# Scaling a tile of integers on VectorE: a product of two tensors, the scale read at stride zero, for the form with a scalar operand

## The reference

```python
def act_qdq(x):
    qmax = 2.0 ** (ACT_BITS - 1) - 1.0
    scale = jnp.maximum(jnp.max(jnp.abs(x)) / qmax, 1e-12)
    return jnp.clip(jnp.round(x / scale), -qmax - 1.0, qmax) * scale
...
x = act_qdq(x)
up = act_qdq(x @ lpbq_dequant(w_up).T)
gate = act_qdq(x @ lpbq_dequant(w_gate).T)
sig = fixed_qdq_u16(jax.nn.sigmoid(gate))
gate = act_qdq(gate * sig)
o = act_qdq(gate * up)
return o @ lpbq_dequant(w_down).T
```

## Time and profile before

| | us |
|---|---|
| median of three runs | 1259.4 |
| lowest and highest | 1258.11, 1260.34 |
| the profiled execution | 1256.11 |
| its span in the trace | 1254.3 |
| around the span | 1.8 |

### The profile page before, as it was taken

How to read it: one execution, slowest core, us unless ns; L and a number is a source line. 1 busy time by engine, 2 the same in 40 slices (tenths; PEclk the granted TensorE clock), 3 DMA queues, 4 the chain that set the end, 5 groups by cost and what they waited for, 6 DMA issues and landing times. The chain is left out here.

```text
span 1254.3 us, 28844 instructions
## 1 busy us (share of the span) xinstructions
PE 1137.2 (91%) x8658; PEld 843.2 (67%) x8658; DVE 1070.1 (85%) x2303; ACT 934.0 (74%) x3155; POOL 448.1 (36%) x463
## 2 busy tenths in 40 slices
PE   1589999999999999999999999999975998989498
PEld 1456666666667666766666766666543988778498
DVE  6259999999999999999999999999874559989698
ACT  1368888888888888888888888888742569855595
POOL 0223334433334433333433333443110007767343
PEclk9899999999999999999999999999986999999799
DMA  5000000000100000100000100010000000000133
GB/s 165 23 17 27 28 22 21 21 21 23 34 22 20 20 20 20 34 24 20 20 20 20 30 29 20 20 33 22 5 4 8 1 1 0 1 1 1 32 104 99
DMA packets 35059, 32.85 MB, mean 26 GB/s; under 512 B 4164, under 2 KB 34748, under 8 KB 35004
## 3 DMA queue, kind: packets, MB, share of 16 engines
q1 hardware_dynamic: 32704, 31.50, 8.4%
q10 hardware_dynamic: 2300, 0.66, 0.3%
HBM read 24.81 MB, written 7.34 MB: 26 GB/s over the span
## 5 line engine op out<-in xcount | busy, mean ns | idle before, releaser
L593 ACT ACTIVATE Px<-score 125x896 f32<-125x896 f32 x128 | 117.4, 917 | 89.4 <-PE score L1121 89.4
L574 ACT ACTIVATE Ps<-score,nmax_s 112x112 f32<-112x112 f32 x512 | 176.3, 427 | 4.0 <-DVE nmax_s L797 4.0
L585 ACT ACTIVATE Px<-score,nmax_h 125x112 f32<-125x112 f32 x512 | 172.6, 367 | 0.8 <-DVE nmax_h L790 0.8
L790 DVE TENSOR_REDUCE nmax_c<-score 125x8 f32<-125x896 f32 x128 | 136.2, 1064 | 13.6 <-PE score L1040 10.4
L574 ACT ACTIVATION_READ_ACCUMULATOR Ps<-score,nmax_s 112x1 f32 x512 | 144.3, 282 | 0.0
L759 DVE TENSOR_REDUCE Zc<-Px 125x8 f32<-125x896 f32 x128 | 137.9, 1077 | 5.7 <-ACT Px L593 2.1
L504 POOL TENSOR_TENSOR Kbd_hi<-Ks_hi,mask 128x448 fp32r<-128x448 f32 x64 | 63.9, 999 | 202.9 <-PE score L1040 137.5
L1132 PE MATMUL outX<-Px,Vn 125*32 125x224 f32 x1536 | 113.6, 368 | 7.2 <-DVE Vn L773 7.2
L585 ACT ACTIVATION_READ_ACCUMULATOR Px<-score,nmax_h 125x1 f32 x512 | 113.0, 221 | 0.0
L525 POOL TENSOR_TENSOR rstd<-vare,half 112x1 f32<-112x1 f32 x64 | 35.1, 548 | 177.0 <-DVE vare L882 177.0
L531 POOL TENSOR_TENSOR xb<-x_in,abo 112x256 f32<-112x256 f32 x32 | 23.7, 739 | 200.2 <-DVE r L868 200.2
(11 more groups left out here) (244 smaller groups left out, 3638.2 us busy)
## 6 DMA issues: line engine op xcount, KB each, us to landing
ctx_in<-in_ctx SPq DMA_DIRECT2D x32, 375.0 KB
x_in<-in_x SPq DMA_DIRECT2D x32, 112.0 KB, 2.0
x_scratch<-x SPq DMA_DIRECT2D x32, 112.0 KB, 1.9
x2T_all<-x_scratch SPq DMA_DIRECT2D x32, 112.0 KB, 2.1
out<-x2T_all SPq DMA_DIRECT2D x32, 112.0 KB, 1.9
raw_w_up<-in_w_up SPq DMA_DIRECT2D x1, 768.0 KB, 5.6
raw_w_down<-in_w_down SPq DMA_DIRECT2D x1, 768.0 KB, 7.4
raw_w_gate<-in_w_gate SPq DMA_DIRECT2D x1, 768.0 KB, 9.5
```

What stands on the lines that cost most here:

```text
L574: ins = act.activation(Ps[:, g, :], score[slot][0:L, h // QUAD, (h % QUAD) * L:(h % QUAD + 1) * L], ACT.Exp, bias=nmax_s[:, g:g + 1], accu ...
L585: ins = act.activation(Px[u % 2][:, h, :], score[SLOT_OF[f"C{u}"]][0:C, h // QUAD, (h % QUAD) * L:(h % QUAD + 1) * L], ACT.Exp, bias=maxim ...
L593: act.activation(Px[u % 2][:].rearrange("s (q h) l -> s q (h l)", q=2), score[SLOT_OF[f"C{u}"]][0:C, :, 0:QW], ACT.Exp).then_inc(exp_c, 1)
L790: dve.tensor_reduce(dst, score[SLOT_OF[f"C{u}"]][0:C, :, 0:QW].rearrange("s q (h l) -> s q h l", h=QUAD), AX.X, ALU.max, negate=True).then ...
```

## The change

In `glu_integers` DVE multiplies the tile by `glu_inv`, a column with one value for each partition. Before, that column is the scalar operand of a `tensor_scalar`. Now it is the second input of a `tensor_tensor`, an operand of the tile's shape that reads the same element again and again at stride zero. Both inputs and the output lie in SBUF; the types (int32 from `U`, f32 from `glu_inv`, int32 to `glu_q`), the wait and the semaphore stay.

```diff
             def glu_integers(g, h):
                 wait(dve, h_done, g * 2 + (h - 1))
-                dve.tensor_scalar(glu_q[h], half_of(products_of_U, g, h), tiny["glu_inv"][:, 0:1], None, ALU.mult)\
-                    .then_inc(glu_q_done, 1)
+                dve.tensor_tensor(glu_q[h], half_of(products_of_U, g, h),
+                                  tiny["glu_inv"][:, 0:1].rearrange("p (o n) -> p o n", o=1).broadcast_to([P, HG, GT]),
+                                  ALU.mult).then_inc(glu_q_done, 1)
```

## The result

The changed kernel takes 1269.87 us, the median of four runs (1269.3 to 1271.32); the kernel before took 1258.76 beside it (1257.91 to 1260.34). The ratio is 1.0089, with a 95% interval of 1.0071 to 1.0106: 11.1 us slower. The forecast was 1270.6 us: 1259.4, the median of the three runs known then, plus 11.2. With a fourth run that median is 1258.76.

The account below looks back on a forecast made before the run. The prediction took POOL and DVE in strict turns to bound the hidden pass. 14 steady tiles at 0.71 us (9.9) and +1.3 for the first two made +11.2, so 1259.4 became 1270.6 us, range 1266.5 to 1274.5.

Parts of the forecast that it names:

- The chain: Hidden pass: POOL and DVE take strict turns, 3.10 us POOL, 0.71 DVE, 0.19 handover, 4.00 a tile.
- The moving time: DVE's product in the hidden pass: moving part doubles from 0.70 to 1.40 us; 1.56 us alone.
- Standing behind POOL: Hidden pass: DVE's product, both inputs in SBUF, waits for POOL's instruction to end, then moves; chance 0.87.
- The sum: Hidden pass: 14 steady tiles at 0.71 us make 9.9, the first two tiles +1.3, in all +11.2 us.
- the first pair: DVE's products of tiles 0 and 1 in the hidden pass: together +1.3 us.
- POOL's first instruction: POOL's first product in the hidden pass: about 4.4 us long after the change.
- the granted clock near 1.00: PE in the hidden pass: new pauses about 1.0 us, so no fall of the clock expected.
- The first rival: Hidden pass: DVE's product runs beside POOL and PE becomes the bound; 9.2 us less, 1250.2 us; chance 0.05.
- PE can start tile 2 when ACT has read tile 0: Start of the hidden pass, if DVE runs beside POOL: PE begins tile 2 at 1103.66.
- The pace: PE in the hidden pass, if DVE runs beside POOL: 3.72 us a tile.
- ACT and PE wait for POOL more than before: Hidden pass: both wait longer but lose nothing; PE stands about 1.0 us of every 4.71.
- the second rival: Hidden pass: DVE and POOL share; -0.19 to +0.71 us a tile, halfway +0.3, 1264 us; chance 0.05.

Follow-up runs that it names:

- e3: Changed kernel with each DVE product preceded by the same product written to a spare place, doubling what DVE moves; 1292.8 us.
- e8: Changed kernel with four buffers in place of two for the integers of the up products; 1271.87 us, ratio 1.0105 to the kernel before.
- e9: Kernel before with four buffers in place of two for the integers of the up products; 1258.7 us, ratio 1.0006.
- e1: Changed kernel with the scale copied once into a PSUM word and read there at stride zero; 1251.88 us, ratio 0.9951 to the kernel before.
- e6: Changed kernel with POOL's product replaced by one of 24 elements and three fills, hidden tensor not computed; one run, 1254.72 us.
- e7: Scale read from PSUM, plus four buffers in place of two for the up products' integers; 1251.33 us, ratio 0.9939 to the kernel before.
- e5: Kernel before with POOL's product replaced by one of 24 elements and three fills, hidden tensor not computed; one run, 1258.7 us.
- e2: Changed kernel with the scale copied once into a full SBUF tile and read at stride one; 1270.07 us, ratio 1.0094 to the kernel before.

## Why the prediction was right, point by point

- **The chain** of POOL and DVE in turn, read from the earlier trace rows, held in all kernels with both inputs in SBUF: e3 shows that added time on DVE appears in full, e8 and e9 that ACT's room counts for nothing.
- **The moving time**: 1.56 us alone was forecast from the earlier trace rows, 1.549 to 1.551 measured; 1.42 behind POOL, 1.43 measured.
- **Standing behind POOL**: read from the short product Vn and taken over to an instruction ten times as long. e1 (the same instruction with one input elsewhere) and e6 (the same instruction beside a POOL that only writes) show that both inputs in SBUF and POOL's reading are what it takes.
- **The sum**: a gap of 1.61 was forecast for the loop, 1.60 measured, from 0.90 (1.49 from 0.79 in the tiles written out, which I had put with the others). 14 tiles x 0.70 is 9.8, the first pair 3.02 in place of 1.74 gives 1.28 (half of it ahead of POOL's first instruction, half within it): 11.1 in all. POOL's instructions in the loop were some 0.02 shorter, which leaves the 10.8 of the pass. 75.5 was forecast for the stretch. The medians differ by 11.1; part of that agreement is luck, as the stages around the pass differ by 2.4 us between the two profiled executions alone.
- **POOL's first instruction**: about 4.4 forecast, 4334 ns measured. POOL's idle time: 31 and 30.8.

Four readings were off, none of which entered the sum.

- I expected the granted clock near 1.00 in the pass. The pauses within the loop did leave it there, but I missed the one at the start. PE stood longer, for 3.26 us (1.98 before): ACT had to wait until POOL's lengthened first instruction had freed a buffer, at 1113.95, and only then emptied the bank and converted the next `x`. The clock then fell to 0.83 and 0.74 in two stretches of 4 us. It cost nothing, as PE had slack (e8, where PE has no such pause, takes as long). The pause and the clock in the changed kernel:

```profile
1117.23 0.46 PE L1634 MATMUL gbank<-xq_hi,w_upT_hi 128*128 128x448 f32 x1 [3.26 <-ACT xq_lo L1445]
...
1112.00:1116.00 4.00, 1.98 (x10) 1.51 (x9) 2.02 (x2) 1.96 (x2) 4.00 (x2) 1.00 0.00 0
1116.00:1120.00 4.00, 2.77 (x11) 2.51 (x12) 4.00 (x3) 2.42 (x3) 2.51 (x2) 0.83 0.00 0
1120.00:1124.00 4.00, 4.00 (x17) 3.66 (x16) 4.00 (x2) 1.18 (x1) 2.51 (x2) 0.74 0.00 0
```

- The first rival, L1573 beside POOL, is real (e1), but its price was too high: 9.2 us forecast, 6.6 in the pass, 5.8 between the medians. The step that failed is "PE can start tile 2 when ACT has read tile 0". PE was then still at tile 1, at the lower clock (1.7 us late in e7's profile), and in e1 it later stood for 2.37 us for ACT, which waited for a buffer that POOL's first instruction held. The pace erred the other way: 3.72 a tile, read from the gate pass, was 3.61 in e1, some 1.5 us less over 14 tiles.
- "ACT and PE wait for POOL more than before" holds for ACT's sum, yet the page now names ACT as the one that POOL waits for. I had not foreseen that and would have been misled by it, had I not had e8.
- The low end of the second rival, -0.19 a tile with PE as the bound, has no working: 3.72 - 4.00 is -0.28. Halfway to +0.71 that is 0.2 a tile and 1262, not 1264.

## What to carry to other kernels

Where VectorE and GpSimd work on SBUF at the same time, look at whether an instruction's duration is its work or its standing: compare it with the same instruction while the other engine is idle, and see how long after the other's end it ends. Trading a scalar operand for a tensor operand to get out of the two-at-a-time form frees nothing here as long as both inputs lie in SBUF and GpSimd reads SBUF at the same time. Putting the small operand into PSUM does free it: the kernel is then 0.5% faster than with the scalar form and 1.4% faster than with the product of two SBUF tensors, although the instruction alone takes 1.55 us and not 0.91. When two engines take turns, price a change by its moving part alone, and measure by the length of the stage, which for one chain held to 0.1 us (75.16, 75.15, 75.23 and 64.33, 64.31) where whole runs spread over 2 to 6. And test a releaser before you believe it: give the engine named more room and see whether the wait goes.

## What the runs showed of the hardware

- A product with its second input in PSUM at stride zero takes 1.545 us for 1344 elements, as fast as with both in SBUF (1.549), and never stands behind POOL (e1).
- A product of two SBUF tensors passes POOL's fills without delay (1.548 us in the median, 1.553 at most, e6), while the scalar form stands behind them, up to 2.77 us (e5).
- The scalar form does not get its turn by having come first. In e5 the one taken up at 1113.77 ended at 1116.17, 0.71 after the end of the last of POOL's fills, although one of those was taken up only at 1114.72:

```profile
1113.77 2.40 DVE L1578 TENSOR_SCALAR up_q<-U,glu_inv 128x1344 int32<-128x1344 int32 x1
...
1113.57 1.22 POOL L1434 MEMSET up_q<- 128x1344 f32 x1
1114.72 0.74 POOL L1435 MEMSET w_down<- 128x768 f32 x1
```

  In the case shown earlier it did get in between two fills. What decides between the two stays open.
- Copying the column to a full tile at stride zero took 1.55 us for 1344 f32 elements (e2), one element at a time, though a copy has a single input in SBUF.
- Matmuls of 448 columns start 0.200 or 0.207 us apart, both at a granted clock of 1.00. The same stage runs at the one pace in one kernel's profile and at the other in the next (gate pass, 990 to 1000: 0.200 after, 0.207 before), for a reason that no run here shows.
